# A fused four-layer kernel on one core: the third layer's gain and residual add, moved from GpSimd to VectorE in all batches

## What is computed

```python
def _L2_xattn_ref(q, k, v, ig_kernel, ig_bias, fg_kernel, fg_bias, outnorm_weight):
    ...
    C = qk * D
    normalizer = jnp.maximum(jnp.abs(C.sum(-1, keepdims=True)), jnp.exp(-max_log_D))
    h = jnp.einsum('bnst,bntd->bnsd', C / (normalizer + EPS_BACKEND), vh)
    h = h.transpose(0, 2, 1, 3)
    mean = h.mean(-1, keepdims=True)
    var = h.var(-1, keepdims=True)
    hn = (h - mean) * jax.lax.rsqrt(var + NORM_EPS) * outnorm_weight
    return hn.reshape(B, S, E)
...
x = x + _L2_xattn_ref(_layernorm(x, axis=-1), ctx_1024, ctx_1024, ...)
x = x + _L2_ffn_ref(_layernorm(x, axis=-1), ...)
```

## Time and profile before

| what | value |
|---|---|
| median of 3 runs | 1398.53 us (1395.99 to 1401.62) |
| profiled execution, its own time | 1400.19 us |
| its span in the trace | 1398.1 us |
| mean granted clock of TensorE in it | 0.973 of full |
| busy in the span: PE, DVE, ACT, POOL | 90%, 61%, 34%, 33% |
| third layer's windows in the trace | about 784 to 960 us |

### The profile page before, as it was taken

How to read it: one execution, slowest core, us unless ns; L and a number is a source line. 1 busy time by engine, 2 the same in 40 slices (tenths; PEclk the granted TensorE clock), 3 DMA queues, 4 the chain that set the end, 5 groups by cost and what they waited for, 6 DMA issues and landing times. The chain is left out here.

```text
span 1398.1 us, 31670 instructions
## 1 busy us (share of the span) xinstructions
PE 1258.8 (90%) x9966; PEld 1008.9 (72%) x9966; DVE 852.8 (61%) x2809; ACT 474.4 (34%) x1119; POOL 463.3 (33%) x435
## 2 busy tenths in 40 slices
PE   5899799997899998899999888897899998899995
PEld 4677589995566665789887666686566665799995
DVE  5788544445577876444575476755567776465563
ACT  3555211112556554011111244453556654111110
POOL 1145612223134334423122256533134343222231
PEclk9999899999999999999999998999999999999998
DMA  9101234422111401464655100000001011646523
GB/s 312 66 17 36 93 103 139 136 65 80 34 36 40 164 33 51 140 205 149 198 174 168 28 8 1 1 1 24 8 17 48 32 40 53 207 100 150 145 46 87
DMA packets 87556, 120.07 MB, mean 86 GB/s; under 512 B 11248, under 2 KB 64752, under 8 KB 87152
## 3 DMA queue, kind: packets, MB, share of 16 engines
q1 hardware_dynamic: 48656, 55.20, 12.9%
q10 hardware_dynamic: 25632, 34.85, 7.6%
q0 software_dynamic: 13152, 28.54, 7.2%
HBM read 82.53 MB, written 38.13 MB: 86 GB/s over the span
## 5 line engine op out<-in xcount | busy, mean ns | idle before, releaser
L1349 PEld LDWEIGHTS bank<-f_xT,f_up 128*128 128x128 f32 x2144 | 253.6, 192 | 13.3 <-issue 6.3
L1349 PE MATMUL bank<-f_xT,f_up 128*128 128x128 f32 x2144 | 258.5, 276 | 2.4 <-DVE f_xT L1225 2.1
L415 DVE TENSOR_REDUCE mha_nmax<-bank 128x2 f32<-128x512 f32 x256 | 170.0, 686 | 117.2 <-PE bank L558 93.5
L1358 PE MATMUL bank<-f_down,f_hT 128*128 128x256 f32 x832 | 199.5, 382 | 4.4 <-DVE f_hT L1266 2.3
L308 ACT ACTIVATE l_took<-bank 128x512 f32<-128x512 f32 x256 | 139.0, 598 | 129.8 <-PE bank L566 129.8
L558 PE MATMUL bank<-l_took,mha_q 32*128 32x256 f32 x1024 | 146.3, 402 | 34.5 <-DVE mha_nmax L415 22.1
L1358 PEld LDWEIGHTS bank<-f_down,f_hT 128*128 128x128 f32 x832 | 149.4, 190 | 24.8 <-DVE f_hT L1266 4.6
L1114 POOL DMA_INDIRECT yout<-f_y,f_to x66 | 81.1, 1229 | 244.9 <-DVE f_y L1302 107.0
L558 PEld LDWEIGHTS bank<-l_took,mha_q 32*128 32x128 f32 x1024 | 90.1, 186 | 74.5 <-DVE mha_nmax L415 45.0
L566 PE MATMUL bank<-l_took 32*128 32x256 f32 x1024 | 142.8, 400 | 0.7 <-ACT l_took L308 0.7
L1165 ACT ACTIVATE f_hT<-bank,f_b 128x128 f32<-128x128 f32 x148 | 46.4, 364 | 276.0 <-PE bank L1349 276.0
(11 more groups left out here) (293 smaller groups left out, 2284.9 us busy)
## 6 DMA issues: line engine op xcount, KB each, us to landing
l_took<-rows SPq DMA_DIRECT2D x91, 132.0 KB
f_up<-in_W ACTq DMA_DIRECT2D x23, 512.0 KB, 4.8
f_down<-in_W ACTq DMA_DIRECT2D x18, 512.0 KB, 5.4
l_took<-rows SPq DMA_DIRECT2D x21, 264.0 KB
f_up<-in_W SPq DMA_DIRECT2D x9, 512.0 KB, 7.3
ring<-yout SPq DMA_DIRECT2D x8, 512.0 KB, 3.9
mha_ctxT<-in_ctxT SPq DMA_DIRECT2D x16, 256.0 KB, 2.9
f_down<-in_W SPq DMA_DIRECT2D x6, 512.0 KB, 7.5
```

Of the source, the lines that this page charges most:

```text
L415: vector.tensor_reduce(nmax[:, p, :, at], ps_s[n % 2][:, :].rearrange("p (k s) -> p k s", s=S), AX.X, ALU.min).then_inc(max_ready, 1)
L1349: ins = pe.matmul(into, up[q][i][:, c, m * P:(m + 1) * P], xT[:, c, :], start=c == 0, stop=c == DC - 1)
L1358: ins = pe.matmul(ps_y[:, 0:D], hT[:, m, :], down[q][:, m, :], start=m == 0, stop=m == HC - 1)
```

## The change

POOL's `finish` loses its multiply and its add for the seven batches that still had them there; it keeps the root. DVE's `finish`, until now only called in the last window, is called in each window with a batch, between `scale` and `tops`.

```diff
                 pool.tensor_tensor(root[:, :, :].rearrange("p k n -> p (k n)"), total[:, :, :].rearrange("p k n -> p (k n)"),
                                    G.mhalf(TPB * HEADS), ALU.pow).then_inc(root_ready, 1)
-                if b == B - 1:
-                    return
-                pool.wait_ge(h_ready, b + 1)
-                pool.tensor_tensor(h[:, :, :], h[:, :, :], out_gain[:, :].unsqueeze(1).to_broadcast([P, TPB, D]),
-                                   ALU.mult).then_inc(gained, 1)
-                pool.wait_ge(gained, b + 1)
-                x = X[:, pair(b), :]
-                pool.tensor_tensor(x, x, h[:, :, :], ALU.add).then_inc(added, 1)
...
                 if now:
                     scale(w_)
-                if w_ == B - 1:
+                if now:
                     finish(w_)
                 if more:
                     tops(w_ + 1)
```

## The result

The changed kernel takes 1418.01 us (median of four runs, 1409.15 to 1421.49), beside 1398.76 for the kernel before on the same chip: a ratio of 1.0131, with an interval of 95% from 1.0101 to 1.0160. It is slower, as forecast, but by 19 us instead of 10, and outside the range of 1401 to 1414. Two later timings of the same kernel gave 1.0127 (1.0095 to 1.0158) and 1.0096 (1.0059 to 1.0134). Over all 22 of its executions the mean is 1412.7 us (spread, as a standard deviation, 5.2), over 74 of the kernel before 1398.5 (3.1): 14.2 us apart.

What follows compares the result with a forecast made beforehand. It took two chains ending together at the hand-overs as the bound, PE's (`outputs`, score product, gates) ending last. Lateness of 7.2 plus clock falls of 3.2 gave +10.4 on 1398.53, so 1409 us, range 1401 to 1414.

Steps and rivals of the forecast that it cites:

- The change's own sum: Third layer's hand-overs: 4.4 + 2.3 + 1.0 - 0.5 = +7.2 us without the clock, +3.2 for new falls, +10.4 in all.
- The three hand-overs at which `z_rows` waited before: Hand-overs 1 to 2, 2 to 3, 3 to 4: all of the 1.46 us delay of `out` passes, 4.4 us.
- Hand-overs 4 to 5 and 5 to 6, with the new falls: 1.15 us of lateness each, PE having 0.31 to spare, plus a new clock fall at 1.6 us each.
- 6 to 7: Last hand-over: PE's second score product had waited 0.49 us for DVE, so 1.46 - 0.49 = 1.0 us passes.
- 0 to 1: First hand-over, no `outputs` yet: later `tops` delays the gates by 0.7, earlier `z_rows` returns up to 1.04; taken as -0.5 us.
- a hold for a whole POOL instruction: DVE's multiply or add beside a working POOL: upper bound 0.69 + 1.27 us; 0.69 was taken, POOL idling there.
- Total: Last step: +10.4 us added to the profiled execution's 1400.19 gives 1410.6, to the median's 1398.53 gives 1408.9; forecast 1409.
- (d): Longer lows of PE's clock, staying through a second stretch at the hand-overs: +15.6 us, 1414.1; chance 0.13.
- (c): DVE's wait for POOL at the statistics decides, not PE: 0.68 us saved in seven hand-overs, -4.8, 1393.7; chance 0.06.
- (b): PE's clock holds at all hand-overs, the three old falls included: +1.4 us, 1399.9; chance 0.08.
- (a): No new fall of PE's clock at the hand-overs, lateness alone: +7.2 us, 1405.7; chance 0.18.

Runs made afterwards that it cites:

- before_fill: The kernel before with two unused products on PE ahead of each window's transposes and one ahead of each score product from the second window; 1396.65 us, ratio 0.9980.
- after_fill2: The changed kernel with two unused products on PE ahead of each window's transposes and four ahead of each score product from the second window; 1409.04 us, ratio 1.0075.
- after_beside_fill2: The changed kernel unaltered, timed and traced again beside the version with both fills; 1409.54 us, ratio 1.0096.
- behind_late: The changed kernel with DVE's multiply and add behind `outputs`, and POOL's `f_add` waiting until DVE's add is done; 1396.41 us, ratio 0.9977.
- behind_outputs: The changed kernel with DVE's multiply and add behind `tops` and `outputs` instead of ahead of them; 1397.89 us, ratio 0.9990.

## Why the prediction was right in direction and too low

**The change's own sum held.** Scale to scale, in us, in four kernels without and with the fills (the window's number is that of the first scaling):

| window | 0 | 1 | 2 | 3 | 4 | 5 | 6 | sum |
|---|---|---|---|---|---|---|---|---|
| before | 21.48 | 21.94 | 22.96 | 21.83 | 17.73 | 16.85 | 16.21 | 139.00 |
| after | 20.27 | 23.40 | 23.34 | 24.18 | 21.00 | 19.35 | 17.02 | 148.56 |
| difference | -1.21 | +1.46 | +0.38 | +2.35 | +3.27 | +2.50 | +0.81 | +9.56 |
| predicted | -0.5 | +1.46 | +1.46 | +1.46 | +2.75 | +2.75 | +1.0 | +10.4 |
| `before_fill` | 20.74 | 20.75 | 20.77 | 20.76 | 17.75 | 17.95 | 16.92 | 135.64 |
| `after_fill2` | 21.48 | 21.75 | 21.75 | 21.76 | 20.34 | 19.32 | 18.22 | 144.62 |

- `out` 2.20 behind the scaling, multiply and add at 0.69, statistics at 2.80: as predicted, to the hundredth.
- The three hand-overs at which `z_rows` waited before: 4.4 predicted, 4.19 measured in these two traces, 4.9 between the means of all. Single ones are off, because the clock's low lasts 6.8 us in window 2 of before and in window 3 of after, and 3.4 in the other.
- Hand-overs 4 to 5 and 5 to 6, with the new falls: 5.5 predicted, 5.77 measured. The falls came, at 902 and 926. The price of one can be read from window 5, in `after_beside_fill2` without a fall and in `after` with one:

```profile
916.64:934.34 17.70, 16.60 (x129) 13.52 (x128) 12.66 (x37) 9.23 (x20) 3.61 (x3) 1.00 0.00 1
922.07:941.42 19.35, 18.24 (x129) 13.79 (x128) 12.68 (x37) 9.23 (x20) 3.61 (x3) 0.91 0.00 1
```

The fall costs 1.65, predicted 1.6, and the lateness alone 0.85 (17.70 against 16.85), predicted 1.15.
- 6 to 7: 1.0 and 0.81. 0 to 1: -0.5 and -1.21; of this, 0.74 is a fall at 810 us in the kernel before that the change lost (21.48 less the 20.74 of `before_fill`), so -0.47 is the hand-over's own.
- The terms are less separate than the prediction has them. At the high clock throughout, a hand-over of 1 to 4 is only 1.0 longer (21.75 against 20.75), not 1.46; with a fall in both it is about 1.4. The clock makes the delay dearer also where it had fallen before. So 4.4 came out by luck: the lateness was put too high there, and the clock, for which the sum had no term at these three, made up for it. As an estimate from these windows, the clock has about half of the 10.3: 1.9 in windows 1 to 3 (4.9 less three times 1.0), 1.65 in window 5, and about as much in window 4.
- In the earlier trace rows the multiply beside L2201 is POOL's for the experts' sums (L1940, 864.43 to 865.69), not the one that moved. What was read from it, a hold for a whole POOL instruction, doesn't hang on that.

**The step that failed is the last, "Total".** It set the sum of one layer equal to the difference of two medians, and so put all that lies outside the layer at nothing. The layer came out as summed, 10.3 us on the mean. In the traces the whole follows it (10.3 in the stretch, -1.3 in the rest and -0.3 around the span, 8.7 in the times: 1409.7 and 1401.0), but over all executions the means are 14.2 apart, and the first four executions had a median of 1418.01, 6 us above the median of all 22, 1411.92, and 1412 is inside the range. So of the 9 us between forecast and result, about 6 are the spread of this kernel's executions, which is bad luck, and the remaining 3, nearly the 4 us that the mean has beyond the stretch, are the part whose cause is open. In the traced one of the first four, 1415.34, the stretch is 9.57 longer than in the first trace of the kernel before, and the rest 5.89 longer. The range was built from cases inside the third layer only and ended at rival (d), 1414.1. It had no term for the rest, which in 20 traces of these kernels went from 1236 to 1252 us, nor for the larger spread of the changed kernel, 5.2 against 3.1. The three runs that the prediction started from lay 5.6 us apart, which was reason enough for such a term.

**The rivals.** (c), that DVE's wait for POOL decides, is out for this change: the wait vanished and the time grew. With `out` punctual, the moment of the statistics does decide, as the windows of 20.29 to 21.02 in `behind_late` and `behind_outputs` show. (b), the clock holding everywhere, is out, as it fell at each of five hand-overs. Its price of +1.4 isn't tested cleanly: `after_fill2`, where all but one fall is gone, is 6.6 us over the kernel before in the stretch, but that has the fall in it and the cost of the fills themselves, 1.2 at 0 to 1 (21.48 against 20.27) and 1.8 in windows 5 and 6 of `before_fill`. (a) and the forecast differ by the new falls, which came. (d), longer lows, happened at 3 to 4 and 4 to 5 and was set off in part by a long low in the kernel before, from 847.9.

## What to carry to other kernels

Work that moves to an engine with spare time is costed by what stands behind it in that engine's queue: here the same 1.4 us of work per pass cost nothing measurable behind one instruction, and some 1 to 3 us per pass ahead of it. Find the instruction that another engine waits for, and put new work behind it; then look whether it overlaps there with another engine's work that holds it up, as `f_add` did (1.64 instead of 0.69). And a sum read from one layer predicts that layer: the range for the whole time needs its own term, from how far the rest of the kernel varies between executions.

## What was not expected of the hardware

- Two adds, DVE's and POOL's, that overlap took 1.64 us each, where they take 0.69 and 1.27 apart: the ends fit one standing still for the other, and then the other for it.
- A clock that is kept up is not time won: `before_fill` holds 1.00 over 135.64 us where the kernel before has 0.94, and the whole gains 0.2% (interval 0 to 0.4). Against the first trace it wins 5.2 us in windows 0 to 3 and loses 1.8 in windows 5 and 6, where the fills stand in the way (17.95 and 16.92 against 16.85 and 16.21).
- Equal programs differ by 10 us in parts that nothing in them changed: in nine traces of the changed kernel the third layer's first scaling came at 800 to 810 us, with 27 to 48 us of low clock before it.
